# Graph attention and a mixture of experts in one kernel: VectorE does the blocks' work ahead of the edges' at five places, the search for the two best experts and one gelu move

## The chip, the cores and the metric

The kernel runs on one core of a Trainium2 chip. The metric is the device time of one execution in microseconds, the median of several runs.

## The reference

6250 nodes with 256 features, 100,000 edges sorted by target. Layer norm, attention over the edges with 4 heads (softmax by target), a product with W_out, and a residual. Then a layer norm, a router that picks 2 of 8 experts, and the experts' two products with a gelu between, all of them computed for every node and weighed:

```python
h = jnp.einsum('ni,hid->nhd', x, W)
e = jnp.einsum('ehd,hd->eh', h_src, a_src) + jnp.einsum('ehd,hd->eh', h_dst, a_dst)
e = jnp.where(e > 0, e, 0.2 * e)
alpha = jnp.exp(jnp.minimum(e - e_max[dst], 20.0))
out_h = segment_sum(alpha / (alpha_sum[dst] + 1e-08) * h_src, dst)
...
rw, re = jax.lax.top_k(jax.nn.softmax(tokens @ router_w.T), 2)
for e in range(8):
    h = jax.nn.gelu(tokens @ w1[e] + b1[e], approximate=False)
    out = out + combine[:, e:e + 1] * (h @ w2[e] + b2[e])
```

## The kernel before

A first phase (to about 91 us) normalizes x, builds the table of rows h and cuts the edges into tiles of 128 that never cross a block of 125 nodes. There are 832 tiles in 52 batches of 16.

The second phase is one loop over batches `it`, from -1 to 57, with 16 **places** `k` in each. Every engine runs through the same places in its own program, and its order is that of the code: no scheduler reorders it. Two kinds of work are woven at each place:

- **Edges**, for batch b = it + 1 and batch `it`. On VectorE: `front` (place 2), `inside` (3), `across` (5), `whole` (7), `argument` (9) make the stable exponent of each edge, in turns with small TensorE products (lines 1115, 1118, 1124 and 1125, 1128); `onehot` (line 793) at places 4, 6, 8 and 15; at 10 `transposed_onehot` (line 786); at 11 to 14 `message(0)` to `message(3)` (line 858), which multiply gathered rows by the exp that ScalarE makes at place 10 (lines 1399 to 1401); at 15 `rescale`. TensorE aggregates one tile of batch `it` a place (line 1150), and ScalarE evacuates the bank of the tile before and clears the next (lines 1382, 1384). GpSimd gathers rows three batches ahead (line 750).
- **Blocks**, from batch 7 on. Groups of three blocks of nodes take a **turn** of three batches, that is 48 **slots** s: 0 to 15 in its first batch, 16 to 31 in its second, 32 to 47 in its third. Expert e has slots 6e to 6e + 5. On TensorE: two hidden products (line 1177) and three output products (line 1223, blocks 0, 1, 2 at slots 6e + 1, 3, 4). On ScalarE a gelu (line 1408) for each hidden product, in general in the same slot. On VectorE an accumulation (line 987) for each output product. Meanwhile the next group is prepared: `divide` at slot 8, `residual` 13 and 19, `variance` 21, `norm` 24 (needs `rstd` from GpSimd, line 756), transposes on TensorE (line 1229) at 11, 17, 29, 31, `split_x` (line 933) 29 and 31, router products 35, `best_two` 36, `differences` 37, `combine` 47. For the last five groups `behind` puts all this six slots later, but for `combine` and, there, the router's exp at slot 47.

On TensorE, ScalarE and GpSimd the blocks' work of a place is in the same pass as the edges'. On VectorE it comes one place late: at place k it does `edges(it, k)` and then the blocks' work of place k - 1. Engines meet by semaphores that count, and some stand for another: L1124 (place 7) waits for the one-hot of place 6, L1128 (place 9) for that of place 8, L1107 (place 0) for that of place 15. The output product of expert e, block 0, waits for the accumulation of expert e - 1, block 2, since both use the bank `ob0`; the transposes at slot 29 wait for the accumulation of slot 27 (bank `ob1`). A tile's aggregation waits until the bank of three tiles before is cleared.

ScalarE holds one table of functions. `table_of_exp` (line 1395) loads that of exp at place 9, the first gelu after place 10 loads that of gelu again, and `LATE` says by how many slots some gelus come after their hidden product:

```python
GELUS = [s for s in range(3 * BT) if s % 6 in (0, 2)]
LATE = {26: 2, 42: 1, 44: 2}
```

Of the kernel before, what the change touches and what calls it, by code (L numbers as in the profile page):

```python
# [19 lines left out]
BT = 16  # L20


def gnn_ffn_kernel(nc, x, src, dst, W, attn, W_out, rw, w1, b1, w2, b2, out):
# [25 lines left out]
    size = lambda g: min(GB, NB - g * GB)  # L49
# [20 lines left out]
    with ExitStack() as ctx:  # L70
# [500 lines left out]
        with ExitStack() as st:  # L571
# [104 lines left out]
            behind = lambda g: 6 if g >= 12 else 0  # L676
# [5 lines left out]
            with nc.Block() as block:  # L682
# [84 lines left out]
                def _(dve):  # L767
# [67 lines left out]
                    def argument(b):  # L835
                        dve.wait_ge(S["rT"], b + 1)
                        v.tensor_tensor(arg[:, :], eC[:, :], rT_ps, ALU.subtract).then_inc(S["arg"], 1)
# [15 lines left out]
                    def message(b, q):  # L853
# [3 lines left out]
                        al = alpha_ps[:, 4 * H * q:4 * H * (q + 1)].rearrange("p (k h) -> p k h", h=H).unsqueeze(3)  # L857
                        v.tensor_tensor(m, m, al.to_broadcast([P, 4, H, DH]), ALU.mult).then_inc(S["msg"], 1)  # L858

                    def edges(it, k):  # L860
                        b = it + 1
                        if k == 6 and 0 <= it < NBAT:
                            onehot(it, 3)
                        if b >= NBAT:
                            return
                        if k == 1 and b >= 1:
                            bank_of_first(b)
                        if k in (4, 8):
                            onehot(b, {4: 0, 8: 1}[k])
                        if k == 15:  # L870
                            onehot(b, 2)
                            if b >= 1:
                                rescale(b)
                        if k == 2:
                            front(b)
                        elif k == 3:
                            inside(b)
                        elif k == 5:
                            across(b)
                        elif k == 7:  # L880
                            whole(b)
                        elif k == 9:
                            argument(b)
                        if k == 10 and b + 1 < NBAT:
                            transposed_onehot(b + 1)
                        if 11 <= k <= 14:
                            message(b, k - 11)
# [45 lines left out]
                        v.tensor_tensor(cols(xTl), ob1[:, 0:n * KC * Q].rearrange("p (b k c) -> p b k c", k=KC, c=Q), cols(xTh),  # L933
                                        ALU.subtract).then_inc(S["ul"], 1)

                    def best_two(g):
                        n = size(g)
                        dve.wait_ge(S["rt"], g + 1)
                        v.tensor_reduce(lg[0:Q, 0:n, :], ob1[0:Q, 0:2 * n * NE].rearrange("p (b t e) -> p b e t", t=2, e=NE), AX, ALU.add).then_inc(S["lgc"], 1)
                        dve.wait_ge(S["lgc"], g + 1)  # L940
                        for i in range(n):
                            v.max(top[0:Q, i, :], lg[0:Q, i, :]).then_inc(S["tops"], 1)
                        dve.wait_ge(S["tops"], 2 * GB * g + n)
                        for i in range(n):
                            v.max_index(topi[0:Q, i, :], top[0:Q, i, :], lg[0:Q, i, :]).then_inc(S["tops"], 1)
                        dve.wait_ge(S["tops"], 2 * GB * g + 2 * n)
# [63 lines left out]
                    def prepare(g, s):  # L1010
                        if s == 8:
                            divide(g)
                        elif s == 13:
                            residual(g, 0)
                        elif s == 19 and size(g) == 3:
                            residual(g, 1)
                        elif s == 21:
                            variance(g)
                        elif s == 24:
                            norm(g)  # L1020
                        elif s == 29:
                            split_x(g, 0)
                        elif s == 31 and size(g) == 3:
                            split_x(g, 1)
                        elif s == 36:
                            best_two(g)
                        elif s == 37:
                            differences(g)

                    v.tensor_copy(iota_ps, iotaR[:, :]).then_inc(S["init"], 1)  # L1030
# [47 lines left out]

                    for it in range(-1, LAST):
                        for k in range(BT):  # L1080
                            edges(it, k)
                            blocks(*((it, k - 1) if k > 0 else (it - 1, BT - 1)))
                    blocks(LAST - 1, BT - 1)

                @block.tensor
# [262 lines left out]
                def _(act):  # L1348
# [40 lines left out]
                        A.copy(acc[:, NB - 1, :], agg_ps[:, (NB - 1) % AB, 0:ROW]).then_inc(S["ev"], 1)  # L1389

                    GELUS = [s for s in range(3 * BT) if s % 6 in (0, 2)]
                    LATE = {26: 2, 42: 1, 44: 2}

                    def table_of_exp():
                        A.activation(warm2[:, :], zc[0:1, 0:1], ACT.Exp).then_inc(S["wm"], 1)  # L1395
# [44 lines left out]
                    for it in range(-1, LAST):  # L1440
                        p, s0 = place(it)
                        for k in range(BT):
# [15 lines left out]
                            s = s0 + k  # L1458
                            if p + 1 < GROUPS:
                                prepare(p + 1, s - behind(p + 1))  # L1460
                                if s == 3 * BT - 1 if behind(p + 1) else s == 42:
                                    router(p + 1)
                            if s == 1 and 0 <= p < GROUPS:
                                weights(p)
                            for at in GELUS:
                                if at + LATE.get(at, 0) == s:
                                    e, f = at // 6 + 1, at % 6 // 2
# [31 lines left out]
```

## Time and profile before

| | |
|---|---|
| median of 3 runs | 1460.2 us (1459.2 to 1461.4) |
| profiled execution | 1459.0 us, its span 1457.2 |
| TensorE busy | 1306.5 us, 90% |
| VectorE busy | 1100.9 us, 76% |
| ScalarE busy | 984.1 us, 68% |
| GpSimd busy | 843.1 us, 58% |
| one turn (L1107 to L1107, 798.83 to 871.49) | 72.7 us |

Busy shares are means over stages. TensorE waits in long stretches before about 290 us; from 400 to 1330 us it is busy 97 to 98% of the time, and single short waits are all that is left. Since the modelled end of a matmul may lie behind the start of the next, the distance between starts tells more than the idle time.

### The profile page before, as it was taken

The page shows a single profiled execution, that of the slowest core. Times are in us where ns is not written, and L with a number is a line of the kernel's source. Part 1 is how long each engine was busy: PE and PEld are TensorE (multiplying, and loading weights), DVE is VectorE, ACT ScalarE, POOL GpSimd, SP SyncE. Part 2 cuts the span into 40 slices and gives each one's busy share as a digit, 9 for nine tenths or more (in the row PEclk, how much of TensorE's full clock was granted, in tenths as well). Part 3 has the DMA queues.
Part 4 walks back from the last instruction along what each step waited for, and adds up shares of the span by engine and source line. Part 5 has one row for each costly group of instructions (what it writes and reads, how often), then busy time and mean ns, then how long its engine had stood idle before and what let it go on. Part 6 is the DMA issues. An engine that isn't in the chain of part 4 may idle for free.

```text
span 1457.2 us, 24806 instructions
## 1 busy us (share of the span) xinstructions
PE 1306.5 (90%) x7177; PEld 1095.0 (75%) x7177; DVE 1100.9 (76%) x3059; ACT 984.1 (68%) x2522; POOL 843.1 (58%) x886
## 2 busy tenths in 40 slices
PE   5933666699999999999999999999999999999997
PEld 3722444588888888888888888888888888888886
DVE  6735765788888888888888888888887888787543
ACT  3723655567676777777777777777777868787723
POOL 1337777766666666666666666666666656570000
PEclk9966777699999999999999999999999999999999
DMA  9564654443444444444444444444444443474000
GB/s 221 154 186 132 167 174 131 117 129 109 137 110 135 111 134 113 132 114 131 115 130 114 131 117 128 116 130 117 128 117 129 115 129 110 133 93 63 6 13 18
DMA packets 89790, 174.52 MB, mean 120 GB/s; under 512 B 22472, under 2 KB 56082, under 8 KB 89626
## 3 DMA queue, kind: packets, MB, share of 16 engines
q0 software_dynamic: 40448, 111.89, 29.9%
q1 hardware_dynamic: 48103, 60.78, 14.0%
q8 instruction: 60, 0.98, 0.3%
q14 instruction: 73, 0.59, 0.1%
q10 hardware_dynamic: 1106, 0.27, 0.1%
HBM read 159.26 MB, written 14.43 MB: 119 GB/s over the span
## 4 chain that ended last, share of the span: by engine, by line
PE 54%; DVE 16%; ACT 13%; issue 5%; POOL 4%; ACTq 1%; DMA 1%; DVEq 0%; POOLq 0%
PE ob L1223 15%; PE agg_ps L1150 15%; PE hb L1177 13%; POOL ring L750 4%; ACT agg_ps L1384 3%; DVE ring L858 3%; ACT acc L1382 3%; PE ob L1259 3%; ACT L1395 2%; DVE oh L793 2%; DVE y L987 2%; ACT hT L1408 2%; PE ob L1229 1%; PE kbank L1107 1%; DVE xn L926 1%
## 5 line engine op out<-in xcount | busy, mean ns | idle before, releaser
L750 POOL DMA_INDIRECT ring<-table,srcE x832 | 811.1, 975 | 412.1 <-issue 208.9
L1150 PE MATMUL agg_ps<-ring,oh 128*128 128x260 f32 x1664 | 515.6, 410 | 1.5 <-ACT agg_ps L1384 1.5
L1382 ACT COPY acc<-agg_ps x831 | 307.0, 369 | 210.7 <-PE agg_ps L1150 130.9
L1223 PE MATMUL ob<-w_sb,hT 128*125 128x256 f32 x1600 | 409.3, 381 | 10.5 <-DVE y L987 10.3
L1223 PEld LDWEIGHTS ob<-w_sb,hT 128*125 128x125 f32 x1600 | 295.7, 187 | 65.4 <-issue 21.4
L1384 ACT COPY agg_ps<-zc 128x260 f32 x832 | 314.6, 378 | 28.6 <-issue 2.3
L1150 PEld LDWEIGHTS agg_ps<-ring,oh 128*128 128x128 f32 x1664 | 300.0, 200 | 40.3 <-ACT agg_ps L1384 3.1
L858 DVE TENSOR_TENSOR ring<-ring,kbank 128x1024 f32<-128x1024 f32 x208 | 244.7, 1214 | 40.9 <-ACT ring L1400 40.6
L987 DVE SCALAR_TENSOR_TENSOR y<-ob,cmb,y 125x256 f32<-125x256 f32 x400 | 188.7, 475 | 56.1 <-PE ob L1223 50.9
L1408 ACT ACTIVATE hT<-hb,b_sb 128x375 f32<-128x375 f32 (+1 forms) x272 | 153.9, 566 | 113.8 <-PE hb L1177 113.2
L1177 PE MATMUL hb<-xTh,w1l 128*128 128x376 f32 (+1 forms) x544 | 181.2, 414 | 7.0 <-ACT hT L1408 6.4
L793 DVE TENSOR_TENSOR oh<-kbank,relE 128x512 f32<-128x512 f32 x208 | 140.8, 677 | 0.8
L1177 PE MATMUL hb<-xTl,w1h 128*128 128x376 f32 (+1 forms) x544 | 136.5, 332 | 0.0
L1177 PE MATMUL hb<-xTh,w1h 128*128 128x376 f32 (+1 forms) x544 | 135.8, 331 | 0.0
L1177 PEld LDWEIGHTS hb<-xTh,w1l 128*128 128x128 f32 x544 | 97.4, 190 | 37.8 <-ACT hT L1408 24.7
L1177 PEld LDWEIGHTS hb<-xTh,w1h 128*128 128x128 f32 x544 | 97.6, 189 | 0.0
L1177 PEld LDWEIGHTS hb<-xTl,w1h 128*128 128x128 f32 x544 | 97.2, 189 | 0.0
L756 POOL TENSOR_TENSOR rstd<-mv,root_ 125x3 f32<-125x3 f32 (+1 forms) x17 | 14.8, 870 | 116.9 <-DVE mv L920 116.9
L1408 ACT ACT_TABLE_LOAD x50 | 64.2, 1283 | 1.7 <-PE hb L1177 0.8
L485 PE MATMUL bank<-wcat,xnT 128*125 128x264 f32 x200 | 54.9, 399 | 5.0 <-DVEq L325 2.9
L807 DVE TENSOR_TENSOR_SCAN FRP<-flags,kbank 64x128 f32<-64x128 f32 x52 | 21.4, 411 | 50.0 <-PE kbank L1115 49.9
L1107 PE MATMUL kbank<-d,OT 128*128 x832 | 29.0, 169 | 33.5 <-DVE oh L793 20.9
(284 smaller groups left out, 1374.4 us busy)
## 6 DMA issues: line engine op xcount, KB each, us to landing
OT<-relb_d SPq DMA_DIRECT2D x52, 512.0 KB
ring<-table,srcE POOLq DMA_INDIRECT x832
y<-in_x_dram SPq DMA_DIRECT2D x50, 125.0 KB
out_dram<-y SPq DMA_DIRECT2D x50, 125.0 KB
table<-hrow SPq DMA_DIRECT2D x25, 227.5 KB
acc<-in_x_dram SPq DMA_DIRECT2D x2, 1568.0 KB
acc<-in_L_ffn_w_dram SPq DMA_DIRECT2D x1, 2048.0 KB, 12.2
w_sb<-in_L_ffn_w_dram SPq DMA_DIRECT2D x1, 2048.0 KB, 12.7
```

What stands on the lines that cost most here:

```text
L485: m = T.matmul(bank[2 + b % 3][0:Q, 0:WIDE], xnT[:, b % 2, k, :], wcat[:, k, :], start=k == 0, stop=k == KC - 1)
L750: pool.indirect_dma_start(out=rings[b % RING][:, k, :], out_offset=None, in_=table[:, :], in_offset=bass.IndirectOffsetOnAxis(ap=srcE[:, t ...
L793: v.tensor_tensor(oh[:, (4 * b + q) % OHQ], iota_ps.unsqueeze(1).to_broadcast([P, 4, P]), relE[:, t0:t0 + 4].unsqueeze(2).to_broadcast([P, ...
L858: v.tensor_tensor(m, m, al.to_broadcast([P, 4, H, DH]), ALU.mult).then_inc(S["msg"], 1)
L987: v.scalar_tensor_tensor(y[0:Q, u, i, :], o[0:Q, 0:D], cmb[0:Q, u, i, e:e + 1], y[0:Q, u, i, :], ALU.mult, ALU.add).then_inc(S["ya"], 1)
L1150: T.matmul(bank_of[k // 8][k % 8], oh[:, (4 * b + q) % OHQ, k % 4, :], rings[b % RING][:, k, :], start=False, stop=True, skip_group_check= ...
L1177: t = T.matmul(out_, a, b_, start=j == 0, stop=j == len(terms) - 1)
L1223: t = T.matmul(o[0:Q, 0:D], hT[:, e % 2, f, cols], w2_sb[:, e, f, :], start=f == 0, stop=f == KC - 1)
L1259: t = T.matmul(ob1[0:Q, j * D:(j + 1) * D], oT[:, j, k, :], wout_sb[:, k, :], start=k == 0, stop=k == KC - 1)
L1382: A.copy(row_of[h][k % 8], closed[h][k % 8]).then_inc(S["ev"], 1)
L1384: A.copy(coming[h][k % 8], zc[:, 0:1].to_broadcast([P, ROW])).then_inc(S["zr"], 1)
L1408: A.activation(hT[:, e % 2, f, 0:w], hb[:, 0:w], ACT.Gelu, bias=b1_sb[:, e, f:f + 1]).then_inc(S["gl"], 1)
```

## The change

Four edits. At places 3, 5, 7, 9 and 11 VectorE does the blocks' work of the place before first and then the edges'. `best_two` is cut: the sum that makes the logits (`logits`) stays at slot 36, the search goes to slot 39 and `differences` from 37 to 40 (for the last five groups all stay where they were). The router's exp goes from slot 42 to 43 on ScalarE. The gelu of the hidden product of slot 26 goes from slot 28 to 27.

```diff
+                    BLOCKS_FIRST = (3, 5, 7, 9, 11)
...
-                    def best_two(g):
+                    def logits(g):
                         n = size(g)
                         dve.wait_ge(S["rt"], g + 1)
                         v.tensor_reduce(lg[0:Q, 0:n, :], ob1[0:Q, 0:2 * n * NE].rearrange("p (b t e) -> p b e t", t=2, e=NE), AX, ALU.add).then_inc(S["lgc"], 1)
+
+                    def best_two(g):
+                        n = size(g)
                         dve.wait_ge(S["lgc"], g + 1)
...
                         elif s == 36:
+                            logits(g)
+                        if s == (36 if behind(g) else 39):
                             best_two(g)
-                        elif s == 37:
+                        elif s == (37 if behind(g) else 40):
                             differences(g)
...
                         for k in range(BT):
-                            edges(it, k)
-                            blocks(*((it, k - 1) if k > 0 else (it - 1, BT - 1)))
+                            if k in BLOCKS_FIRST:
+                                blocks(it, k - 1)
+                                edges(it, k)
+                            else:
+                                edges(it, k)
+                                blocks(*((it, k - 1) if k > 0 else (it - 1, BT - 1)))
...
-                    LATE = {26: 2, 42: 1, 44: 2}
+                    LATE = {26: 1, 42: 1, 44: 2}
...
-                                if s == 3 * BT - 1 if behind(p + 1) else s == 42:
+                                if s == 3 * BT - 1 if behind(p + 1) else s == 43:
```

VectorE, second batch of a turn, places 6 to 10, before: `variance` ends (`mv`), `whole` (`XmP` to `FRP`), the accumulation of slot 22 (`y`), a one-hot, the argument, norm.

```order
L920 SCALAR_TENSOR_TENSOR mv<-stat,mv 125x3
L828 TENSOR_TENSOR XmP<-kbank,kmask 64x32
L829 COPY scA<-kbank 128x4
L830 TENSOR_REDUCE CB<-XmP 64x2
L831 SCALAR_TENSOR_TENSOR FRP<-flags,CB,kbank 64x128
L832 SCALAR_TENSOR_TENSOR FRP<-flags,CB,kbank 64x128
L833 TENSOR_TENSOR FRP<-FRP 64x128
L987 SCALAR_TENSOR_TENSOR y<-ob,cmb,y 125x256
L793 TENSOR_TENSOR oh<-kbank,relE 128x512
L837 TENSOR_TENSOR arg<-eC,kbank 128x64
L926 TENSOR_SCALAR xn<-y,mv,rstd 125x256 x3
L786 TENSOR_SCALAR OT<-OT,pid 128x2048
```

The same place of the changed kernel (its lines are numbered up to five higher; L992 is the accumulation, L928 norm).

```order
L922 SCALAR_TENSOR_TENSOR mv<-stat,mv 125x3
L992 SCALAR_TENSOR_TENSOR y<-ob,cmb,y 125x256
L828 TENSOR_TENSOR XmP<-kbank,kmask 64x32
L829 COPY scA<-kbank 128x4
L830 TENSOR_REDUCE CB<-XmP 64x2
L831 SCALAR_TENSOR_TENSOR FRP<-flags,CB,kbank 64x128
L832 SCALAR_TENSOR_TENSOR FRP<-flags,CB,kbank 64x128
L833 TENSOR_TENSOR FRP<-FRP 64x128
L793 TENSOR_TENSOR oh<-kbank,relE 128x512
L928 TENSOR_SCALAR xn<-y,mv,rstd 125x256 x3
L837 TENSOR_TENSOR arg<-eC,kbank 128x64
L786 TENSOR_SCALAR OT<-OT,pid 128x2048
```

The accumulation went ahead of `whole`, norm ahead of the argument. VectorE, third batch, around places 8 and 9, before: the end of `whole`, a one-hot, the accumulation of slot 39, the argument, the accumulation of slot 40.

```order
L833 TENSOR_TENSOR FRP<-FRP 64x128
L793 TENSOR_TENSOR oh<-kbank,relE 128x512
L987 SCALAR_TENSOR_TENSOR y<-ob,cmb,y 125x256
L837 TENSOR_TENSOR arg<-eC,kbank 128x64
L987 SCALAR_TENSOR_TENSOR y<-ob,cmb,y 125x256
L786 TENSOR_SCALAR OT<-OT,pid 128x2048
```

The same place of the changed kernel.

```order
L833 TENSOR_TENSOR FRP<-FRP 64x128
L793 TENSOR_TENSOR oh<-kbank,relE 128x512
L992 SCALAR_TENSOR_TENSOR y<-ob,cmb,y 125x256
L947 MAX top<-lg 125x8 x3
L950 MAX_INDEX topi<-top,lg 125x8 x3
L992 SCALAR_TENSOR_TENSOR y<-ob,cmb,y 125x256
L956 CAST topf<-topi 125x6
L957 TENSOR_TENSOR dif<-lg,top 125x3x8
L958 TENSOR_TENSOR dif<-top 125x3x2
L960 TENSOR_TENSOR cmb<-picks,topf 125x24
L961 TENSOR_TENSOR cmb<-picks,topf 125x24
L837 TENSOR_TENSOR arg<-eC,kbank 128x64
```

Search and differences now stand between the one-hot and the argument. ScalarE, second batch, places 11 to 13, before: evacuation, register loads of addresses (`tabs`), evacuation, the gelu with its table load, evacuation.

```order
L1382 COPY acc<-agg_ps 128x260
L1384 COPY agg_ps<-zc 128x260
L659 TENSOR_LOAD tabs
L664 ISA x3
L1382 COPY acc<-agg_ps 128x260
L1384 COPY agg_ps<-zc 128x260
L1408 ACT_TABLE_LOAD
L1408 ACTIVATE hT<-hb,b_sb 128x375
L1382 COPY acc<-agg_ps 128x260
L1384 COPY agg_ps<-zc 128x260
```

The same place of the changed kernel (L1393 and L1395 evacuate and clear, L1419 is the gelu).

```order
L1393 COPY acc<-agg_ps 128x260
L1395 COPY agg_ps<-zc 128x260
L1419 ACT_TABLE_LOAD
L1419 ACTIVATE hT<-hb,b_sb 128x375
L659 TENSOR_LOAD tabs
L664 ISA x3
L1393 COPY acc<-agg_ps 128x260
L1395 COPY agg_ps<-zc 128x260
L1393 COPY acc<-agg_ps 128x260
L1395 COPY agg_ps<-zc 128x260
```

The gelu with its table load went ahead of the register loads and of one evacuation.

## Rows read from the trace of the kernel before

**Rows 1.** Waits of TensorE, 400 to 1330 us: total us, times, longest

```profile
PE ob L1223 <- DVE y L987: 8.9, 22, 0.6
PE kbank L1124 <- DVE oh L793: 4.8, 13, 0.4
PE hb L1177 <- ACT hT L1408: 4.2, 12, 0.6
PE kbank L1107 <- DVE oh L793: 2.2, 3, 0.8
```

**Rows 2.** Timeline of TensorE, first batch of turn 7: start us, length us

```profile
814.99 0.60 PE L1150 MATMUL agg_ps<-ring,oh 128*128 128x260 f32 x2
815.43 0.59 PE L1229 MATMUL ob<-ident,xn 125*128 125x125 f32 x4
815.86 0.61 PE L1150 MATMUL agg_ps<-ring,oh 128*128 128x260 f32 x2
816.11 0.70 PE L1177 MATMUL hb<-xTh,w1l 128*128 128x376 f32 x2
...
817.34 0.60 PE L1150 MATMUL agg_ps<-ring,oh 128*128 128x260 f32 x2
818.10 1.10 PE L1223 MATMUL ob<-w_sb,hT 128*125 128x256 f32 x4 [0.16 <-DVE y L987]
```

**Rows 3.** Timeline of TensorE, second batch of turn 7, places 9 to 14

```profile
837.09 1.10 PE L1223 MATMUL ob<-w_sb,hT 128*125 128x256 f32 x4 [0.54 <-DVE y L987]
...
842.65 0.60 PE L1150 MATMUL agg_ps<-ring,oh 128*128 128x260 f32 x2
843.31 0.65 PE L1229 MATMUL ob<-ident,xn 125*128 125x125 f32 x4
843.80 0.61 PE L1150 MATMUL agg_ps<-ring,oh 128*128 128x260 f32 x2
844.34 0.61 PE L1177 MATMUL hb<-xTh,w1l 128*128 128x376 f32 x2
```

**Rows 4.** Timeline of VectorE, same batch: the accumulation of slot 27

```profile
842.78 0.47 DVE L987 SCALAR_TENSOR_TENSOR y<-ob,cmb,y 125x256 f32<-125x256 f32 x1
```

**Rows 5.** Timeline of GpSimd, same batch

```profile
835.07 0.88 POOL L756 TENSOR_TENSOR rstd<-mv,root_ 125x3 f32<-125x3 f32 x1 [1.93 <-DVE mv L920]
```

**Rows 6.** Timeline of ScalarE, same batch, places 10 to 12

```profile
840.11 0.30 ACT L1400 ACTIVATE ring<-arg 128x64 f32<-128x64 f32 x1
...
842.42 1.28 ACT L1408 ACT_TABLE_LOAD   x1
843.72 0.57 ACT L1408 ACTIVATE hT<-hb,b_sb 128x375 f32<-128x375 f32 x1
```

**Rows 7.** Timeline of TensorE, third batch of turn 7, place 7

```profile
858.53 0.41 PE L1124 MATMUL kbank<-CCP,picks 128*128 128x32 f32 x2 [0.42 <-DVE oh L793]
```

**Rows 8.** Timeline of VectorE, same batch, places 5 to 8

```profile
856.90 0.31 DVE L942 MAX8 top<-lg 125x8 f32<-125x8 f32 x3
...
857.78 0.69 DVE L793 TENSOR_TENSOR oh<-kbank,relE 128x512 f32<-128x512 f32 x1
...
858.78 0.15 DVE L951 CAST topf<-topi 125x6 f32<-125x6 uint32 x1
...
859.57 0.18 DVE L828 TENSOR_TENSOR XmP<-kbank,kmask 64x32 f32<-64x32 f32 x1
...
861.76 0.47 DVE L987 SCALAR_TENSOR_TENSOR y<-ob,cmb,y 125x256 f32<-125x256 f32 x1
```

**Rows 9.** Timeline of ScalarE, same batch, place 10: the exp

```profile
863.92 0.22 ACT L1399 ACTIVATE kbank<-arg 128x64 f32<-128x64 f32 x1
```

**Rows 10.** Timeline of TensorE, turn 12, start of its third batch

```profile
1213.21 0.56 PE L1107 MATMUL kbank<-d,OT 128*128 x16
```

**Rows 11.** Timeline of VectorE, turn 12, end of its second batch

```profile
1212.13 0.69 DVE L793 TENSOR_TENSOR oh<-kbank,relE 128x512 f32<-128x512 f32 x1
```

**Rows 12.** Timeline of VectorE, batch 5, before the first turn

```profile
258.60 0.80 DVE L926 TENSOR_SCALAR xn<-y,mv,rstd 125x256 f32<-125x256 f32 x2 [12.89 <-POOL rstd L756]
```

## The prediction

> **What bounds the kernel now.** I read the waits of TensorE over 400 to 1330 us first, where the pattern repeats: four sorts of wait, about 20 us of 930 together [rows 1]. TensorE runs close to its end-to-end bound, so a change of order on VectorE can give back only waits. That view misses short ones: the end of a matmul is modelled, so I then read the order of TensorE's instructions in one turn (48 slots, 798.8 to 871.5 us) and compared steps from start to start. Undisturbed, an aggregation is followed by an fp32 matmul after 0.44 us (814.99 to 815.43) and by a hidden product after 0.25 (815.86 to 816.11) [rows 2]. Larger steps are stalls:
> first batch, place 13, output product: 817.34 to 818.10 = 0.76, so 0.32 lost [rows 2];
> second batch, place 9, output product: 0.54 idle; place 13, transposes L1229: 842.65 to 843.31 = 0.66, 0.22 lost; place 14, hidden product: 843.80 to 844.34 = 0.54, 0.29 lost [rows 3];
> third batch, place 7, L1124: 0.42 idle [rows 7].
> All but the 0.29 are ended by VectorE; that one waits for the gelu of slot 28. Turns 0 to 10 (11 of them) have this pattern; turns 11 to 14 have the preparation six slots later and another one.
>
> **First batch of a turn.** Output of expert 2 needs the accumulation of slot 10, which stands behind message 0, and that waits for ScalarE's exp. Ahead of it, it starts when its own product is done (the aggregation behind that begins at 814.99 [rows 2]) and is over near 815.6, ahead of 817.8. The divide comes in front of the argument; its three instructions fit before the table load that the exp stands behind, so I cost it at nothing; were that cover gone it would cost its length, about 1.3 us by three instructions of this size, estimated. The gelu behind this place is ready in time because the projection (place 13) stands between. Gain 0.32 a turn; bounds 0 and 0.32.
>
> **Second batch.** The accumulation of slot 22 goes in front of `whole`: TensorE's 0.54 at place 9 goes. What is late next? The transposes at place 13 wait for the accumulation of slot 27, which stays behind message 1. It starts at 842.78 [rows 4], and the messages begin when ScalarE's second exp is done: 840.11 plus 0.30 is 840.41 [rows 6], and the change moves neither this exp (it hangs on the gelu of slot 24 and a table load) nor the two messages between. Message 0 started at 840.53, so at most 0.12 can be gained, 0.09 after the hand-over. So of 0.54 plus 0.22 only 0.09 comes through: TensorE arrives earlier at place 13 and stands there instead. Norm in front of the argument needs GpSimd's rstd; that starts at 835.07 and takes 0.88 [rows 5], 1.6 us before norm is reached, so it is covered.
> The gelu of slot 27 now stands right behind the evacuation at place 11; table load and gelu take 842.42 to 844.29 before the change [rows 6] and come out one evacuation with its wait (about 1.3 us) earlier, near 843.0, ahead of the hidden product at 844.05. The 0.29 goes. What is queued behind the gelu is the evacuation of place 12, which moves from 841.6 to about 842.9; TensorE needs its bank only three tiles later, about 3 us on. The next transposes (slot 31) then meet the split of x about 0.06 early. Net 0.09 + 0.29 - 0.06 = 0.32; bounds 0.1 (gelu's cover lost) and 1.05 (all three stalls gone).
> A table load is followed by its activation 1.30 us after its start: 842.42 to 843.72 [rows 6]. The Trainium skill (ScalarE: Activation LUTs, What ACT_TABLE_LOAD costs) adds a drain of 1.38 us to the load, 2.66 in all. By that rule the moved pair would end near 844.4 and the sum be smaller by about 3 us (rival 5). The trace has no such gap, so I go by 1.30.
>
> **Third batch.** Reducing the logits goes in front of `across`, into idle time; the search (856.90 to 857.78, 0.88 us) leaves the way to the one-hot, for which L1124 waits at 858.53 [rows 7, 8]. That clears the 0.42. But search and differences (858.78 to 859.57, 0.79 us) now stand in front of the argument, with the accumulation of slot 40 (0.40). `whole` then starts when its matmuls allow, 0.88 earlier; the accumulation of slot 39 moves from 861.76 [rows 8] to 860.88 and ends at 861.27; plus 0.88, 0.40 and 0.79 the argument starts at 863.34, and the exp can follow when that is written, estimated at 0.26, so at 863.60. The exp ran at 863.92 [rows 9], 0.42 earlier 863.50. So the exp is late by 0.10 and everything behind it, hidden product at slot 45 included: gain 0.42 - 0.10 = 0.32; bounds -0.4 (argument another 0.8 late) and 0.6.
> The router's exp one slot later stays on its side of the table load: nothing.
>
> **Other stretches.** The 13 waits at L1124 [rows 1] are 10 of 0.42 and 3 of 0.17 at a turn's start; the latter go as well: 0.5 in all. In turns 11 to 14 the waits for the gelu are up to 0.6, but behind them the product L1107 needs the one-hot that starts at 1212.13 and takes 0.69 [rows 11]; handed over, L1107 can't start before about 1212.87, against 1213.21 [rows 10]. So 0.34 each, 1.4 in all. At a turn's end search and logits come in front of message 0, into its wait, which clears L1107's three waits (2.2 in all, [rows 1]); next late is the combination, held by the router's exp, so I take 0.33 each, 1.0 in all, bounds 0 and 2.2. At the start norm waits 12.89 us for GpSimd [rows 12], whose queue of gathers sets that time: nothing before 258.6 us counts. There norm now holds back the argument, so the exp ends about when message 0 wants it: 0.2 lost, and up to 1.
>
> **Sum.** 11 turns x (0.32 + 0.32 + 0.32) = 10.6; + 0.5 + 1.4 + 1.0 - 0.2 = 13.3 us. The profiled execution took 1459.0, so 1445.7; it lies 1.2 under the median of the runs, and from 1460.2 the sum gives 1446.9: 1447.
>
> **Rivals.**
> 1. Every stall above stays gone (0.32 + 1.05 + 0.6 a turn, 21.7 us; late turns 2 us each, 8): about 1430. For it: VectorE is idle in the places where work is moved. Against: exp and messages between slots 24 and 27 don't move. Chance 0.08.
> 2. The argument in the third batch is late by more (search, differences and accumulation stand in one row, 2.07 us): 0.35 more a turn takes 3.9 us, and no gain at the turns' ends another 1.5: 1452. Chance 0.17.
> 3. Freed waits all come back at the next exp: only the gelu's 0.23 a turn and 1.5 in the late turns remain, 4 us: 1456. Chance 0.08.
> 4. Slower: norm, now ahead of the argument, waits for rstd also in the steady turns. At the start it waits 12.89 us [rows 12]. If GpSimd takes rstd behind the four gathers of a quad, norm is up to 5 us late; margin 1.6 plus the exp's own 1.2 are covered, so from 2.8 us on it decides, and 5 us late costs 2.2 a turn, 24 us, less 13: 1471. Against: rstd starts on VectorE's word [rows 5], with GpSimd waiting. Chance 0.04.
> 5. The moved gelu comes out a microsecond or more later than its row says, since loading a table costs the activation behind it more than 1.30 us: the 0.29 stays lost, 3.2 us over 11 turns: 1450. Against: every such pair in the trace is 1.30 apart, as 842.42 and 843.72 [rows 6]. Chance 0.03. The page named above states such a cost; the trace disagrees with it.
> The forecast has 0.6. A measurement here tells about 0.2% (3 us) from no change. The range 1437 to 1455 takes in rival 2, and half of what lies between the forecast and rival 1; its own range is 1442 to 1451. Faster: 0.6 + 0.08 + 0.17 + 0.03 and half of rival 3, 0.04, make 0.92; within 0.2%: the other half, 0.04; slower 0.04.
>
> **What would show it.** TensorE idle before the output product at place 9 of the second batch near 0, the step before L1229 at place 13 grown from 0.66 to about 1.0; 0.25 before the hidden product at place 14; no wait at L1124 in the third batch and the argument there waiting for nothing, starting about 0.3 us ahead of the exp; a turn of about 71.8 us for 72.8. I am wrong if L1229 waits no more than now (rival 1), if the argument comes over 0.5 us late for the exp (rival 2), or if norm waits on GpSimd in steady turns (rival 4).

## The result and the profile after

The changed kernel takes **1443.2 us** (median of 4 runs, 1441.8 to 1445.2); the kernel before took 1459.7 beside it (4 runs, 1458.8 to 1461.4). The ratio is 0.9887, 95% interval 0.9869 to 0.9904: 16.5 us faster. The profiled execution took 1441.8 us, its span is 1439.7, against 1457.2.

In the trace the start of each batch is the first matmul of L1107, which is L1118 now. All lines of the later part are higher: L1135 for L1124, L1139 for L1128, L1161 for the aggregation L1150, L1188 for the hidden product L1177, L1234 for the output product L1223, L1240 for the transposes L1229, L1293 and L1299 for router product and weights. A turn takes 71.47 us as a mean of ten (360.11 to 1074.77), for 72.73 before (362.45 to 1089.75).

Waits of TensorE after, 400 to 1330 us: total us, times, longest. It answers to [rows 1].

```profile
PE hb L1188 <- ACT hT L1419: 11.1, 16, 1.4
PE ob L1240 <- DVE y L992: 3.5, 10, 0.4
PE ob L1234 <- DVE y L992: 2.1, 3, 0.7
PE ob L1299 <- DVE cmb L977: 1.9, 3, 0.7
PE kbank L1139 <- DVE oh L793: 1.8, 9, 0.2
PE kbank L1129 <- DVE oh L793: 0.3, 1, 0.3
```

The kernel before had one line more than [rows 1] shows:

```profile
PE ob L1288 <- DVE cmb L972: 0.6, 3, 0.2
```

So the sum did not fall (20.7 us before, 20.7 after) while the kernel lost 16.5. The waits at the output product went from 22 to 3 and those at L1124 are gone; the gelu's grew from 4.2 to 11.1, that for the combination (L1288, now L1299) from 0.6 to 1.9, and the transposes have about one a turn. The gelu's are long and show in this view; many that went were short and show only in part (0.17 of 0.33, below). So what follows is read from start to start.

Batch by batch, before minus after, mean of turns 0 to 10: **first 0.62, second 0.27, third 0.38 us**, 14.0 in all. Turns 11 to 14 gave 2.6. The first turn began 0.98 earlier (288.70 for 289.68).

Timeline of TensorE after, first batch of turn 7 (start us, length us), answering to [rows 2]:

```profile
817.18 0.60 PE L1161 MATMUL agg_ps<-ring,oh 128*128 128x260 f32 x2
817.62 1.03 PE L1234 MATMUL ob<-w_sb,hT 128*125 128x256 f32 x4
```

0.44 from start to start for 0.76: the 0.32 is gone. Second batch of turn 7, answering to [rows 3]:

```profile
831.90 0.60 PE L1161 MATMUL agg_ps<-ring,oh 128*128 128x260 f32 x2
832.86 0.65 PE L1240 MATMUL ob<-ident,xn 125*128 125x125 f32 x4 [0.36 <-DVE y L992]
833.34 0.61 PE L1161 MATMUL agg_ps<-ring,oh 128*128 128x260 f32 x2
833.59 0.70 PE L1188 MATMUL hb<-xTh,w1l 128*128 128x376 f32 x2
```

The output product at place 9 waits for nothing (825.66 to 826.00). The product with the one-hot of place 8, L1139, now waits 0.19, which the prediction had not named; it stands ahead of the exp's gate and that exp starts 15.71 after the batch's start in both kernels, so it costs nothing more. The step before the transposes has grown from 0.66 to 0.96, and the one before the hidden product has shrunk from 0.54 to 0.25. Timeline of VectorE in the same batch, answering to [rows 4], places 11 and 12:

```profile
830.05 2.35 DVE L858 TENSOR_TENSOR ring<-ring,kbank 128x1024 f32<-128x1024 f32 x2 [0.74 <-ACT ring L1411]
832.32 0.48 DVE L992 SCALAR_TENSOR_TENSOR y<-ob,cmb,y 125x256 f32<-125x256 f32 x1
```

Both messages stand ahead of the accumulation at 832.32, for which the transposes at 832.86 wait, and the messages wait 0.74 for ScalarE's exp. ScalarE there, answering to [rows 6]:

```profile
829.72 0.30 ACT L1411 ACTIVATE ring<-arg 128x64 f32<-128x64 f32 x1
...
830.74 1.28 ACT L1419 ACT_TABLE_LOAD   x1
832.04 0.57 ACT L1419 ACTIVATE hT<-hb,b_sb 128x375 f32<-128x375 f32 x1
```

The gelu follows its table load after 1.30 us, as before. The Trainium skill (ScalarE: Activation LUTs, What ACT_TABLE_LOAD costs) puts 2.66 there; neither trace agrees with it. Norm had its input in time: GpSimd's `rstd`, answering to [rows 5], is over at 825.55, and norm starts at 827.08.

```profile
824.67 0.88 POOL L756 TENSOR_TENSOR rstd<-mv,root_ 125x3 f32<-125x3 f32 x1 [1.92 <-DVE mv L922]
```

Third batch of turn 7, places 9 to 13, answering to [rows 8, 9]. VectorE, then ScalarE, then TensorE at slot 45:

```profile
852.47 0.22 DVE L837 TENSOR_TENSOR arg<-eC,kbank 128x64 f32<-128x64 f32 x1
```

```profile
850.75 1.28 ACT L1406 ACT_TABLE_LOAD   x1
...
852.54 0.38 ACT L1395 COPY agg_ps<-zc 128x260 f32 x1
852.85 0.22 ACT L1410 ACTIVATE kbank<-arg 128x64 f32<-128x64 f32 x1
...
854.19 1.28 ACT L1419 ACT_TABLE_LOAD   x1
855.48 0.57 ACT L1419 ACTIVATE hT<-hb,b_sb 128x375 f32<-128x375 f32 x1
```

```profile
854.53 1.03 PE L1234 MATMUL ob<-w_sb,hT 128*125 128x256 f32 x4
856.11 0.61 PE L1188 MATMUL hb<-xTh,w1l 128*128 128x376 f32 x2 [0.55 <-ACT hT L1419]
```

ScalarE goes from the table load through evacuation and clearing to the exp and the gelu; the argument is ready at 852.69 (852.47 and 0.22), 0.16 ahead of the exp. The hidden product then waits for the gelu: 1.58 from start to start, where before it was 1.00 (866.14 to 867.14). Counted from the batch's start, TensorE was 0.93 ahead of the kernel before at the hidden product behind L1139 (13.74 for 14.67) and only 0.36 ahead behind this wait (18.71 for 19.07). Most of what the one-hots gave in this batch is given back here.

In the late turns three waits are new or larger, here in the first batch of turn 12, in its second, and in the first of turn 13:

```profile
1168.81 0.60 PE L1188 MATMUL hb<-xTh,w1l 128*128 128x376 f32 x2 [1.43 <-ACT hT L1419]
1194.96 1.10 PE L1234 MATMUL ob<-w_sb,hT 128*125 128x256 f32 x4 [0.70 <-DVE y L992]
1222.63 0.49 PE L1299 MATMUL ob<-ident,cmb 125*24 125x125 f32 x3 [0.69 <-DVE cmb L977]
```

### The profile page after: what moved, and what is told of

It is laid out like the page before. It is cut to its first block, busy times and chain, and to the rows that moved or that the text cites. A ratio compares the mean times of both kernels' runs of the same rounds, so it can differ in the third digit from the quotient of the medians.

```text
span 1439.7 us, 24809 instructions
## 1 busy us (share of the span) xinstructions
PE 1296.2 (90%) x7177; PEld 1100.6 (76%) x7177; DVE 1097.4 (76%) x3059; ACT 982.1 (68%) x2522; POOL 853.3 (59%) x886
## 4 chain that ended last, share of the span: by engine, by line
PE 59%; ACT 15%; DVE 7%; issue 5%; POOL 5%; ACTq 1%; DMA 1%; DVEq 0%; POOLq 0%
PE agg_ps L1161 18%; PE ob L1234 16%; PE hb L1188 15%; POOL ring L750 5%; ACT agg_ps L1395 4%; ACT acc L1393 3%; ACT L1406 3%; PE ob L1270 3%; ACT hT L1419 3%; DVE ring L858 2%; PE ob L1240 2%; PE kbank L1118 1%; DMA ring<-table,srcE 1%; PE ob L1310 1%; ACTq L664 1%
## 5 line engine op out<-in xcount | busy, mean ns | idle before, releaser
L750 POOL DMA_INDIRECT ring<-table,srcE x832 | 821.4, 987 | 385.1 <-issue 212.3
L1161 PE MATMUL agg_ps<-ring,oh 128*128 128x260 f32 x1664 | 518.2, 413 | 1.6 <-ACT agg_ps L1395 1.4
L1393 ACT COPY acc<-agg_ps x831 | 306.3, 369 | 199.0 <-PE agg_ps L1161 120.6
L1234 PE MATMUL ob<-w_sb,hT 128*125 128x256 f32 x1600 | 407.2, 379 | 2.9 <-DVE y L992 2.8
L1234 PEld LDWEIGHTS ob<-w_sb,hT 128*125 128x125 f32 x1600 | 297.9, 187 | 49.4 <-issue 4.6
L1395 ACT COPY agg_ps<-zc 128x260 f32 x832 | 314.6, 378 | 28.6 <-issue 2.3
L1161 PEld LDWEIGHTS agg_ps<-ring,oh 128*128 128x128 f32 x1664 | 302.2, 201 | 39.9 <-ACT agg_ps L1395 3.9
L992 DVE SCALAR_TENSOR_TENSOR y<-ob,cmb,y 125x256 f32<-125x256 f32 x400 | 189.4, 477 | 83.1 <-PE ob L1234 76.7
L1419 ACT ACTIVATE hT<-hb,b_sb 128x375 f32<-128x375 f32 (+1 forms) x272 | 153.6, 565 | 108.5 <-PE hb L1188 107.7
L1188 PE MATMUL hb<-xTh,w1l 128*128 128x376 f32 (+1 forms) x544 | 183.0, 417 | 14.7 <-ACT hT L1419 13.5
L1188 PE MATMUL hb<-xTl,w1h 128*128 128x376 f32 (+1 forms) x544 | 136.6, 332 | 0.0
L1188 PE MATMUL hb<-xTh,w1h 128*128 128x376 f32 (+1 forms) x544 | 135.7, 331 | 0.0
L1188 PEld LDWEIGHTS hb<-xTh,w1l 128*128 128x128 f32 x544 | 99.0, 190 | 40.8 <-ACT hT L1419 27.0
L1188 PEld LDWEIGHTS hb<-xTh,w1h 128*128 128x128 f32 x544 | 97.5, 188 | 0.0
L1188 PEld LDWEIGHTS hb<-xTl,w1h 128*128 128x128 f32 x544 | 97.4, 189 | 0.0
L1118 PE MATMUL kbank<-d,OT 128*128 x832 | 28.9, 169 | 29.8 <-DVE oh L793 17.0
```

The source lines that it names most:

```text
L750: pool.indirect_dma_start(out=rings[b % RING][:, k, :], out_offset=None, in_=table[:, :], in_offset=bass.IndirectOffsetOnAxis(ap=srcE[:, t ...
L992: v.scalar_tensor_tensor(y[0:Q, u, i, :], o[0:Q, 0:D], cmb[0:Q, u, i, e:e + 1], y[0:Q, u, i, :], ALU.mult, ALU.add).then_inc(S["ya"], 1)
L1161: T.matmul(bank_of[k // 8][k % 8], oh[:, (4 * b + q) % OHQ, k % 4, :], rings[b % RING][:, k, :], start=False, stop=True, skip_group_check= ...
L1188: t = T.matmul(out_, a, b_, start=j == 0, stop=j == len(terms) - 1)
L1234: t = T.matmul(o[0:Q, 0:D], hT[:, e % 2, f, cols], w2_sb[:, e, f, :], start=f == 0, stop=f == KC - 1)
L1393: A.copy(row_of[h][k % 8], closed[h][k % 8]).then_inc(S["ev"], 1)
```

## The experiments

Theory: TensorE is given back only what passes two gates of the second and third batches, the messages behind ScalarE's exp and the gelu behind its table load. A place that is moved alone frees a wait that stands again at the next gate. Rivals: each place gives its own gain; or one of the parts (the gelu, the search) gives nothing.

The first four ran on one chip, with the kernel before at 1459.9 (21 runs).

**One place alone.** The kernel before, with blocks first at place 7 only.

```diff
-                            edges(it, k)
-                            blocks(*((it, k - 1) if k > 0 else (it - 1, BT - 1)))
+                            if k in (7,):
+                                blocks(it, k - 1)
+                                edges(it, k)
+                            else: ...
```

> The kernel before with the blocks' work first at place 7 alone. My theory (the freed wait turns up again at the transposes of slot 29, which hang on the exp): the 0.54 us idle before the output product of slot 25 goes, the step before L1229 grows from 0.66 to about 1.0, and only 0.1 to 0.15 us of a turn is saved: 1 to 2 us in all. Rival (a wait taken away stays away): 0.54 a turn over 11 turns, 6 us.

Measured: 1461.3, ratio 1.0011 (1.0002 to 1.0020). The three batches of a turn save 0.02, -0.01 and 0.00. TensorE there, second batch of turn 7:

```profile
836.19 0.50 PE L1181 MATMUL hb<-xTh,w1h 128*128 128x376 f32 x2
836.53 1.03 PE L1227 MATMUL ob<-w_sb,hT 128*125 128x256 f32 x4
837.75 0.33 PE L1132 MATMUL kbank<-ident,FRP 128*128 128x128 f32 x1 [0.19 <-DVE oh L793]
...
842.43 0.60 PE L1154 MATMUL agg_ps<-ring,oh 128*128 128x260 f32 x2
843.38 0.65 PE L1233 MATMUL ob<-ident,xn 125*128 125x125 f32 x4 [0.35 <-DVE y L987]
843.87 0.61 PE L1154 MATMUL agg_ps<-ring,oh 128*128 128x260 f32 x2
844.49 0.61 PE L1181 MATMUL hb<-xTh,w1l 128*128 128x376 f32 x2
```

The wait of place 9 is gone: its output product follows after 0.34, for 1.04 before (836.05 to 837.09), 0.70 less. Behind it the product with the one-hot of place 8 comes after 1.22 for 0.94 (0.28 given back), the transposes after 0.95 for 0.66 (0.29), the hidden product after 0.62 for 0.54 (0.08). That is 0.65 of the 0.70, over three gates. The mechanism is the one expected, but not even the 0.1 to 0.15 a turn came through.

**Places 7 and 12.** As above, `k in (7, 12)`, which puts the accumulation of slot 27 ahead of message 1.

> The kernel before with the blocks' work first at places 7 and 12, so that the accumulation of slot 27 no longer stands behind message 1. My theory: now both stalls go, 0.54 at place 9 and 0.22 at place 13, 0.7 us a turn less what the gelu of slot 28 takes back (the hidden product behind the transposes waits for it: it is ready at a fixed time, so most of the 0.7 may come back there unless the gelu moves too). If the gelu is the next link, the saving stays near that of place 7 alone plus 0 to 0.2 a turn (2 to 4 us); if nothing else is late, 8 us.

Measured: 1460.9, ratio 1.0007 (0.9998 to 1.0016); no batch of a turn saves 0.02. TensorE there:

```profile
847.88 0.61 PE L1154 MATMUL agg_ps<-ring,oh 128*128 128x260 f32 x2
849.06 0.61 PE L1181 MATMUL hb<-xTh,w1l 128*128 128x376 f32 x2 [0.57 <-ACT hT L1412]
```

The wait for the accumulation is gone, and all of it stands at the gelu: 1.18 from start to start for 0.25. That is 0.93. So these two places can't help in the second batch without the gelu, which is the gate behind them; the 0 to 0.2 a turn that was expected did not come.

**The changed kernel with the gelu back at slot 28.**

```diff
-                    LATE = {26: 1, 42: 1, 44: 2}
+                    LATE = {26: 2, 42: 1, 44: 2}
```

> The changed kernel with the gelu back at slot 28. My theory: 0.23 to 0.29 us a turn lost at the hidden product of slot 30, and up to 0.3 in each of three or four late turns: 3 to 4 us slower than the changed kernel, 1446 to 1447. Rival (the gelu's move is worth nothing, since TensorE stands at the transposes anyway): no difference.

Measured: 1446.6, ratio 0.9906 (0.9891 to 0.9921). The batches save 0.61, -0.02 and 0.36. TensorE there:

```profile
837.24 0.61 PE L1161 MATMUL agg_ps<-ring,oh 128*128 128x260 f32 x2
837.86 0.61 PE L1188 MATMUL hb<-xTh,w1l 128*128 128x376 f32 x2
```

0.62 for 0.25. The whole gain of the second batch, 0.29 a turn or 3.2 us, hangs on this one number: without it all five places together give nothing there. Between the medians, taken on two chips, lie 3.5 us, but the intervals of the two ratios overlap; what shows the loss is the batches. Whether the gelu's move alone would give as much, without any of VectorE's places, is not shown.

**The changed kernel with place 12 too.**

```diff
-                    BLOCKS_FIRST = (3, 5, 7, 9, 11)
+                    BLOCKS_FIRST = (3, 5, 7, 9, 11, 12)
```

> The changed kernel with place 12 added to those at which the blocks' work goes first. My theory: the 0.52 us that TensorE loses before the transposes of slot 29 goes, and with it 4 to 6 us in all (11 turns), to about 1438; the split of x at slot 31 then gives back about 0.1 a turn. Rival (everything behind the exp is paced by the messages, so the next wait takes it all): no difference, 1443.

Measured: 1444.2, ratio 0.9895 (0.9881 to 0.9910). The batches save 0.58, 0.27 and 0.38, about as without it: the 4 to 6 us expected did not come, and the rival is right. TensorE there, slots 31 and 32 of turn 7:

```profile
837.01 1.02 PE L1234 MATMUL ob<-w_sb,hT 128*125 128x256 f32 x4
838.44 0.43 PE L1240 MATMUL ob<-ident,xn 125*128 125x125 f32 x2 [0.41 <-DVE xTl L935]
```

The transposes of slot 29 now follow after 0.44, and those of slot 31 take the wait (1.43 where 0.86 is usual): their bank is freed by the split of x, which stands behind message 3.

**Four parts on another chip.** Search back, the gelu alone, the change without place 9, and place 11 alone.

> The changed kernel with the search at slot 36, the differences at 37 and the router's exp at slot 42, as before the change. My theory: L1124 in the third batch waits about 0.4 us again, 11 turns and the batch before the first turn: 4 to 5 us slower than the changed kernel, about 1448. Rival (moving the search only shifts the wait to the exp behind the argument): no difference.

> The kernel before with the gelu at slot 27 and nothing else. My theory: 0.2 to 0.29 us a turn and 0.3 in each late turn, 3 to 4 us faster than the kernel before. Rival (a gelu ahead of the evacuation delays aggregation): the same or slower.

> The changed kernel with place 9 taken out of the list: divide, norm and the accumulation of slot 40 with the differences stand behind the argument again. My theory: place 9 brings nothing in steady turns (the argument has cover) and costs 0.7 us before the first turn, where norm waits for GpSimd: 0 to 1 us faster than the changed kernel. Rival: the idle time of VectorE that place 9 fills is worth 0.1 to 0.3 a turn, so 1 to 3 us slower.

> The kernel before with the blocks' work first at place 11 alone. My theory: the 0.32 us (with its tail 0.39) before the output product of slot 13 goes in turns 0 to 10, 3.5 to 4.3 us; in the late turns search and logits come ahead of message 0, which brings 0.3 to 0.9 at each of three turn ends: 5 to 6 us faster than the kernel before in all. Rival (it comes back at the exp of the next batch): under 2 us.

On this chip the kernel before took 1610.0 (36 runs) at a mean granted clock of 0.92 where the others had 0.95. The four gave 1622.0, 1617.3, 1606.9 and 1616.0, ratios 1.0067 (1.0034 to 1.0100), 1.0041 (1.0014 to 1.0069), 0.9969 (0.9941 to 0.9996) and 1.0036 (1.0013 to 1.0060). The largest difference in VectorE's waits, over 90 to 1450 us of the first of the four:

```profile
DVE dsum L798 <- remote: 131.1, 41, 25.1
```

L798 adds up what TensorE's first product of a batch (L1107) left in its bank; `remote` says that the profile names nothing that ended these waits. The gathered rows come in three lines later, at L801, whose wait for their transfers is shorter here than in the kernel before (14.2 for 27.5 us). TensorE's granted clock from 400 to 1330 us is 0.97, for 1.00. What makes this chip slower is not known; the kernel before has no trace from it. Since a turn's batches are 23 to 33 us long here, with waits that the other chips don't show, these ratios say nothing sure about the order of a turn's work. They do say that the gain was not to be had on this chip. Only the first question was asked again; the gelu alone and places 9 and 11 by themselves stay open.

The last four ran on one chip, with the kernel before at 1460.9 (9 runs).

**Search back, again.** Its edit on the changed kernel:

```diff
-                        if s == (36 if behind(g) else 39):
+                        if s == 36:
                             best_two(g)
-                        elif s == (37 if behind(g) else 40):
+                        elif s == 37:
...
-                                if s == 3 * BT - 1 if behind(p + 1) else s == 43:
+                                if s == 3 * BT - 1 if behind(p + 1) else s == 42:
```

> The changed kernel with the search back at slot 36, the differences at 37 and the router's exp at 42, while the five places stay as changed. Theory: the argument of the third batch no longer has search and differences ahead, but the one-hot of place 6 has, so L1135 waits 0.42 again and the third batch of a steady turn loses most of the 0.38 that it gained: 4 to 5 us above the changed kernel, about 1448. Rival (the order of places alone gives the third batch's gain, the argument's delay having cost as much as the one-hot's wait): within 2 us of 1443.

Measured: 1445.0, ratio 0.9894 (0.9879 to 0.9909), not told apart from the changed kernel's 0.9887. The batches save 0.61, 0.27 and **0.42**: the third gains a little more than with the search moved. The rival is right in its number. VectorE there, third batch of turn 7, places 5 and 9, then ScalarE's exp:

```profile
846.37 0.19 DVE L941 TENSOR_REDUCE lg<-ob 125x24 f32<-125x48 f32 x1
846.59 0.31 DVE L947 MAX8 top<-lg 125x8 f32<-125x8 f32 x3
...
848.07 0.23 DVE L816 TENSOR_TENSOR_SCAN EX<-masks,EX,kbank 4x16 f32<-4x16 f32 x1 [0.63 <-PE kbank L1129]
...
854.31 0.21 DVE L837 TENSOR_TENSOR arg<-eC,kbank 128x64 f32<-128x64 f32 x1
```

```profile
856.23 0.22 ACT L1410 ACTIVATE kbank<-arg 128x64 f32<-128x64 f32 x1
```

Since place 5 does the blocks' work first, the search runs while VectorE would wait for L1129, and still leaves 0.63 idle. It no longer holds up the one-hot in either kernel. And the exp starts 15.46 after the batch's start here (856.23, batch from 840.77), 15.45 in the changed kernel (852.85, from 837.40), though the argument is ready 1.71 ahead of it here and 0.16 there. So search and differences in front of the argument cost nothing either; the rival's reason, that the argument's delay cost as much as the one-hot's wait, is wrong. In all 11 turns of both kernels, as in the kernel before and in the next one, the exp starts 0.31 behind the start of ScalarE's own clearing (L1395), at the end of table load, evacuation and clearing.

**The table of exp two places earlier.** In the third batch only, with the differences behind the argument.

```diff
-                        elif s == (37 if behind(g) else 40):
+                        elif s == (37 if behind(g) else 41):
...
-                             if k == 9 and it + 1 < NBAT and p is not None:
+                             if k == (7 if s0 == 2 * BT else 9) and it + 1 < NBAT and p is not None:
```

> The changed kernel with the table of exp loaded at place 7 for 9 in the third batch of a turn, and the differences at slot 41 for 40, behind the argument. Theory: in the third batch the argument starts about 0.8 earlier and the exp with it, the gelu of slot 42 (issued at 43) follows, and the 0.83 that TensorE loses ahead of the hidden product at slot 45 shrinks by about 0.5 a turn: 5 us below the changed kernel, 1438. Rival (the hidden product waits for a gelu that hangs on something other than the exp, or the early table of exp makes an additional load for a gelu between): no gain, within 2 us of 1443, or slower by a load, 1.3 a turn, 14 us.

Measured: **1435.1**, ratio 0.9834 (0.9819 to 0.9850), 7.7 us below the changed kernel by the ratios. The third batch saves 0.95 for 0.38. ScalarE and TensorE there, third batch from 834.29:

```profile
849.16 0.22 ACT L1410 ACTIVATE kbank<-arg 128x64 f32<-128x64 f32 x1
```

```profile
851.40 1.03 PE L1234 MATMUL ob<-w_sb,hT 128*125 128x256 f32 x4
852.42 0.61 PE L1188 MATMUL hb<-xTh,w1l 128*128 128x376 f32 x2
```

The exp starts 14.87 after the batch's start, 0.58 earlier, and the hidden product 18.13, also 0.58 earlier. That is the gate of the third batch: ScalarE's chain with its table load, as search back had said. Two things were changed together, and the rows say that both were needed: in the changed kernel the argument is ready only 0.16 ahead of the exp, so by them the earlier table alone could give at most 0.16 of the 0.58. Here the differences stand behind the argument, which is ready 0.40 ahead of the earlier exp. Neither half was run by itself. Of the 6.7 us between the spans, 6.3 are 11 x 0.57; the first batches give back 1.0, the late turns save 1.5 more.

**Places 12 and 14.**

```diff
-                    BLOCKS_FIRST = (3, 5, 7, 9, 11)
+                    BLOCKS_FIRST = (3, 5, 7, 9, 11, 12)
...
-                            if k in BLOCKS_FIRST:
+                            if k in BLOCKS_FIRST or (k == 14 and place(it)[1] == BT):
```

> The changed kernel with place 12 first in every batch, and place 14 first in the second batch of a turn alone, so that the accumulation of slot 27 stands ahead of message 1 and the split of x for slot 29 ahead of message 3. Theory (each product of this chain waits in turn for the next blocks' item that stands behind a message): the 0.56 that TensorE lost at the transposes of slot 31 in the run with place 12 goes, the transposes of slot 29 lose nothing either, so the second batch of a steady turn gains about 0.5 more: 11 turns, 5 to 6 us below the changed kernel, about 1438. Rival (the next item behind them takes the wait, as it did twice): the product behind slot 31 or a place of the following batch loses the 0.5, and the time stays within 2 us of the changed kernel, 1443.

Measured: 1441.0, ratio 0.9865 (0.9844 to 0.9886), not clearly apart from the changed kernel. The second batch does save 0.64 for 0.27, and the wait is gone:

```profile
835.38 1.03 PE L1234 MATMUL ob<-w_sb,hT 128*125 128x256 f32 x4
836.24 0.38 PE L1240 MATMUL ob<-ident,xn 125*128 125x125 f32 x2
```

0.86 for 1.43. That makes 4.0 us over 11 turns, less than the 0.5 a turn expected. But the first turn starts at 291.71 for 288.70, and the other batches give back another 1.0, so the spans are equal (1439.6 and 1439.7).

**Both.** The two edits together.

> Both edits of the two runs above on the changed kernel. Theory: their gains add, since one is in the second and one in the third batch: about 10 us below the changed kernel, 1433. Rival: what one frees the other's stall takes back; then no better than the better of the two.

Measured: 1435.1, ratio 0.9828 (0.9813 to 0.9844). The batches save 0.53, 0.65 and 0.95, so the gains do add in the steady turns; the time doesn't follow, since the first turn starts at 291.46 and the late turns' second batches and ends save 2.0 less than with the early table alone (3 x 0.25 and 3 x 0.42; their first batches give 0.2 back). With place 12 the batch before the first turn took 23.36 us in all three changed kernels that have it, 21.3 to 22.0 in the four without (the changed kernel, gelu back, search back, early table). What is longer there is TensorE's work, not its waits. Stretches from 4 to 8 us after that batch's start, with the early table alone and then with places 12 and 14 (us; busy us of TensorE, its weight loads, VectorE, ScalarE and GpSimd; TensorE's granted clock; DMA share and GB/s):

```profile
271.41:275.41 4.00, 3.24 (x22) 2.66 (x20) 2.90 (x14) 2.23 (x7) 2.98 (x4) 0.98 0.49 143
272.35:276.35 4.00, 4.00 (x19) 3.71 (x17) 1.38 (x5) 1.07 (x4) 2.95 (x4) 0.50 0.48 144
```

In all seven the granted clock is at 0.50 (1.2 GHz) in the last 12 us before this batch, where TensorE stands still for 8 or 9 us in one stretch. In the four without place 12 it is at 1.00 (2.4 GHz) before the fifth us of the batch is over, and is low once more for some us behind its tenth; with place 12 it stays at 0.50 for the first 15 us, though TensorE is busy nearly throughout. Over the whole batch it is 0.66 in the three, with TensorE busy 20.8 us, and 0.77 to 0.82 in the four, with 17.1 to 17.7. So a slower clock makes that batch longer; what holds it down with place 12 is not shown, and each kernel has one profiled execution. The version with the early table alone is the simplest of the fastest.

## Why the prediction was right

Forecast 1447, range 1437 to 1455, measured 1443.2: faster, by 16.5 us for 13.3. By its terms, from the traces of the two profiled executions (their spans are 17.5 us apart; 17.6 are in place by the last batch's start):

| term | forecast | measured |
|---|---|---|
| first batches, 11 | 3.5 | 6.9, with the next term |
| turn starts (L1124 at 0.17) | 0.5 | in the row above |
| second batches, 11 | 3.5 | 3.0 |
| third batches, 11 | 3.5 | 4.1 |
| late turns, second batches | 1.4 | 0.6 |
| late turns, ends | 1.0 | 2.7 |
| late turns, first batches | 0 | -0.7 |
| before the first turn | -0.2 | 1.0 |

**First batch: mechanism right, size short.** Odd turns save 0.42 to 0.47: the 0.32 before the output product, and 0.07 at the step behind it (818.10 to 819.03 before, 817.62 to 818.48 after). Even turns save 0.73 to 0.80. The step that was mis-sized is "3 of 0.17 at a turn's start": it took idle time from the view of waits after warning against it. Timeline of TensorE, first batch of turn 6, before and then after:

```profile
735.18 0.50 PE L1177 MATMUL hb<-xTh,w1h 128*128 128x376 f32 x2
735.85 0.41 PE L1124 MATMUL kbank<-CCP,picks 128*128 128x32 f32 x2 [0.17 <-DVE oh L793]
```

```profile
726.68 0.50 PE L1188 MATMUL hb<-xTh,w1h 128*128 128x376 f32 x2
727.02 0.36 PE L1135 MATMUL kbank<-CCP,picks 128*128 128x32 f32 x2
```

0.67 for 0.34: the listed 0.17 was 0.33. And it is there in all six even turns: the view names three, in the others the step is as long (0.64 in turn 4) and no wait is listed. Six of 0.30 to 0.34 are 1.9, for 0.5.

**Second batch: right in its steps.** It said that of 0.54 and 0.22 only 0.09 comes through at the transposes, their step growing to about 1.0; it is 0.96. It said 0.25 before the hidden product; it is 0.25. Putting the gelu back cost 0.29 a turn. Of the 0.09 of the accumulation 0.07 was there: it starts 18.31 after the batch's start for 18.38, and TensorE is 0.07 ahead at the transposes. But of the 0.29 at the hidden product only 0.20 lasts, since the step behind it is 0.54 now (833.59 to 834.13) and was 0.45 behind the stall (844.34 to 844.79). That makes 0.27 for the 0.32. With the gelu back even the 0.07 is lost in front of the hidden product (the batch saves -0.02).

**Third batch: right sum, wrong reasons.** The text had the search leave the way to the one-hot, which clears 0.42, and then cost 0.10 in front of the argument. Search back showed both false: with place 5 first the search is out of the one-hot's way wherever it stands, and the argument was not what the exp waited for in any steady turn. The step that failed is "the exp can follow when that is written": it left out ScalarE's own chain of table load, evacuation and clearing, which ends at 852.92 in the trace after (852.54 and 0.38), behind the argument's 852.69 (852.47 and 0.22). The 0.42 was too small as well, again because it was taken from the view of waits: the step before L1124 was 0.93 (857.60 to 858.53) and is 0.35 (846.94 to 847.29), 0.58 less. That 0.42 minus 0.10 is near 0.38 is luck; the exp simply came 0.40 earlier from the batch's start (15.85 to 15.45), and TensorE, 0.93 ahead by then, waited for its gelu.

**Late turns and start.** Their sum was 2.4 and is 2.6, by other parts. The ends clear L1107's waits nearly whole (0.78 to 0.98 each for 0.33); what came next was the combination, as the text said: L1299 waits up to 0.69, which puts TensorE 0.38 to 0.47 back at the start of turns 12 to 14. The output product later in these first batches frees more than that, and the gelu behind it takes it back (the 1.43 above, for 0.60), so they lose 0.15 to 0.44. In the second batches the text had L1107 as the next gate, at 0.34. It was the output product ahead of it, which waits for an accumulation (the 0.70 above): in turn 12 TensorE is 0.97 ahead in front of it and 0.21 behind it. Before the first turn norm does wait on GpSimd (14.0 for the 12.89 of [rows 12]), and the argument behind it, but the last batch ahead of the turn takes 21.7 us for 23.4 and it comes out 1.0 ahead. TensorE's granted clock over that batch is 0.81 for 0.75, and the engine is busy 17.46 us for 18.61. The prediction had no such term. This stretch varies most: the kernels here reach their first turn between 288.7 and 294.2 (the latter in an execution 2.9 us above its kernel's median), and the clock goes with it in the runs with place 12.

**Rivals.** 1 fell: the transposes wait more, not less. 2 fell: the argument is not late. 3 is refuted for the whole change, but true of VectorE's places in the second batch as long as the gelu stays, as the first three experiments show. 4 fell: `rstd` is over 1.5 us ahead of norm. 5 fell: 830.74 to 832.04 is 1.30.

## What to carry to other kernels

When engines run in fixed orders, a wait that an edit removes goes to the next gate; follow it through to the last one and price only what passes there. Before costing work put in front of an instruction, look for what that instruction's consumer waits for on its own engine: here ScalarE's chain with the table load set the exp, and moving that load earlier together with the differences gave 7.7 us where moving the search gave nothing. Measure stalls from start to start in the timeline, against the smallest step of the same pair, since the view of waits left out part or all of the short ones (0.17 of 0.33, 0.42 of 0.58, nothing of 0.29), and read on to the next step, which can take some back (0.29 at the hidden product was worth 0.20).

## What the runs showed that was not expected

- Turns alternate: with the same code, even turns saved 0.26 to 0.38 more in their first batch than odd ones, in all of turns 0 to 10. Most of it is the stall in front of L1124, 0.30 to 0.34 in the even turns and 0.04 to 0.06 in the odd ones; why they differ is not known.
- The total of TensorE's listed waits stayed at 20.7 us while the steady stretch got 14 us shorter.
- In the last batch before the first turn TensorE's granted clock is 0.75 to 0.82 in the kernels without place 12 and 0.66 or 0.67 in the four with it, and in each pair the batch is 1.4 to 2.1 us longer with place 12.
- On another chip the kernel before takes 1610 us for 1460, and there three of the four variants were slower than it by 0.36 to 0.67%. The cause is not known.
